# Edges' multiplicity as a logarithm in the logits, maxima of four heads at once, and two of four heads set apart by GpSimd, in a graph attention softmax

## The reference, cut to what matters

```python
x = x * jax.lax.rsqrt(ms + EPS) * rms_w
x = x @ W_down
loop = jnp.arange(n, dtype=edge_index.dtype)
src = jnp.concatenate([edge_index[0], loop])
dst = jnp.concatenate([edge_index[1], loop])
xl = (x @ Wl).reshape(n, H, D)          # H = 4 heads, D = 64
xr = (x @ Wr).reshape(n, H, D)
msg = xl[src] + xr[dst]
act = jnp.where(msg > 0, msg, NEG_SLOPE * msg)
e = jnp.einsum('ehd,hd->eh', act, att)
m = jax.ops.segment_max(e, dst, num_segments=n)
p = jnp.exp(e - m[dst])
denom = jax.ops.segment_sum(p, dst, num_segments=n)
alpha = p / (denom[dst] + 1e-16)
out = jax.ops.segment_sum(alpha[..., None] * xl[src], dst, num_segments=n)
out = out.reshape(n, HID)
return out @ W_up
```

## Time and profile before

| | |
|---|---|
| median of 3 runs | 3800.36 us (3797.71 to 3806.73) |
| the profiled execution | 3811.61 us |
| its span in the trace | 3809.9 us |
| granted TensorE clock, mean | 0.956 of full speed |
| busy: TensorE (matmul) | 3487.1 us, 92% |
| busy: TensorE (weight loads) | 2907.5 us, 76% |
| busy: VectorE | 1925.3 us, 51% |
| busy: GpSimd | 1237.3 us, 32% |
| busy: ScalarE | 904.2 us, 24% |
| chain that ended last | TensorE 60%, DMA 12%, GpSimd 10%, VectorE 7%, issue 6%, ScalarE 4% |
| in it: scatter into EM, its DMA | 6% |
| in it: exponentials L1908 | 2% |

### The profile page before, as it was taken

The page is one execution under the profiler, slowest core; times in us unless marked ns, Lnnn a source line. Parts: engine busy times, 40 slices in busy tenths (PEclk is TensorE's granted clock), DMA queues, the critical chain, the costliest instruction groups (busy, mean ns, idle before and its releaser), DMA issues.

```text
span 3809.9 us, 55179 instructions
## 1 busy us (share of the span) xinstructions
PE 3487.1 (92%) x22747; PEld 2907.5 (76%) x22747; DVE 1925.3 (51%) x4210; ACT 904.2 (24%) x1340; POOL 1237.3 (32%) x947
## 2 busy tenths in 40 slices
PE   5899079999999799999999699999999999999988
PEld 4665058999999799987778596777777777777788
DVE  7864155221333354455545497676764444444467
ACT  0111024111201211221111394332312222222224
POOL 2677633322333027776677562200000000000021
PEclk8999589999999899999999899999999999999999
DMA  8588862556422435455544557442341222221233
GB/s 291 140 263 244 244 201 65 131 126 142 121 59 51 167 102 161 153 169 185 164 145 144 185 218 269 173 139 81 123 141 56 90 76 81 77 87 67 68 100 104
DMA packets 270889, 533.95 MB, mean 140 GB/s; under 512 B 86587, under 2 KB 135730, under 8 KB 268618
## 3 DMA queue, kind: packets, MB, share of 16 engines
q1 hardware_dynamic: 145526, 400.68, 31.0%
q0 software_dynamic: 74080, 52.74, 8.7%
q10 hardware_dynamic: 51030, 77.00, 5.8%
HBM read 352.66 MB, written 177.63 MB: 139 GB/s over the span
## 4 chain that ended last, share of the span: by engine, by line
PE 60%; DMA 12%; POOL 10%; DVE 7%; issue 6%; ACT 4%; SPq 0%; POOLq 0%; ACTq 0%; DVEq 0%
PE ps L393 40%; PE ps L721 14%; DMA EM<-ee,adr 6%; POOL gr L2151 3%; POOL EM L2141 3%; POOL gl L2151 3%; PE ps L483 3%; DMA T<-cnt,adr 2%; ACT pb L1908 2%; DVE eqj L882 1%; POOL T L2114 1%; DVE eqj L879 1%; DMA slab<-T 1%; PE ps L398 1%; ACT pt L1922 1%
## 5 line engine op out<-in xcount | busy, mean ns | idle before, releaser
L721 PE MATMUL ps<-mh,whl 128*128 128x384 f16 (+5 forms) x2560 | 528.5, 300 | 20.3 <-DVE gs L1391 14.4
L393 PE MATMUL ps<-wb,xth 128*128 128x256 f32 (+1 forms) x2560 | 460.8, 282 | 7.1 <-DVE xtl L1056 5.2
L2114 POOL DMA_INDIRECT TR<-cnt,adr x167 | 270.8, 1621 | 541.2 <-DMA TR<-cnt,adr 509.6
L393 PEld LDWEIGHTS ps<-wb,xth 128*128 128x128 f32 (+1 forms) x2560 | 389.2, 186 | 8.1 <-DVE xtl L1056 5.4
L2189 POOL TENSOR_TENSOR graw<-graw,rsb 128x1280 f32<-128x1280 f32 (+1 forms) x2 | 5.6, 2822 | 1166.8 <-DMA graw<-GD 1166.8
L721 PE MATMUL ps<-ml,whl 128*128 128x384 f16 (+5 forms) x1280 | 383.0, 299 | 0.0
L721 PEld LDWEIGHTS ps<-mh,whl 128*128 128x128 f16 (+1 forms) x2560 | 289.1, 117 | 92.7 <-issue 14.5
L393 PE MATMUL ps<-wb,xtl 128*128 128x256 f32 (+1 forms) x1280 | 358.5, 280 | 0.0
L393 PE MATMUL ps<-a,yy 128*128 128x384 f16 (+4 forms) x2560 | 343.7, 297 | 6.5 <-DVE yy L1403 5.2
L393 PE MATMUL ps<-a,xhb 128*128 128x384 f16 (+5 forms) x1280 | 341.0, 296 | 0.0
L393 PE MATMUL ps<-a,xob 128*128 128x384 f16 (+5 forms) x1280 | 339.8, 296 | 0.0
(11 more groups left out here) (308 smaller groups left out, 6974.1 us busy)
## 6 DMA issues: line engine op xcount, KB each, us to landing
TR<-zero_w SPq DMA_DIRECT2D x80, 625.0 KB, 3.8
wraw<-in_L_gnn_weight SPq DMA_DIRECT2D x64, 512.0 KB, 3.3
EM<-neg SPq DMA_DIRECT2D x10, 2500.0 KB, 21.8
ar<-TR SPq DMA_DIRECT2D x72, 320.0 KB
eb<-EM SPq DMA_DIRECT2D x9, 2500.0 KB, 9.1
ar<-TR SPq DMA_DIRECT2D x72, 305.0 KB
UD<-ue ACTq DMA_DIRECT2D x72, 256.0 KB, 3.2
uu<-UD SPq DMA_DIRECT2D x36, 512.0 KB, 6.9
```

Of the source, the lines that this page charges most:

```text
L393: i = pe.matmul(ap, l, r, start=(q == 0), stop=(q == len(pairs) - 1))
L721: ins = pe.matmul(ps[:, 0:cn], l, r, start=(q == 0), stop=(q == len(pairs) - 1))
L2114: return pool.indirect_dma_start(out=flat, out_offset=bass.IndirectOffsetOnAxis(ap=adr[:, n, t:t + 1], axis=0), in_=cnt[:, n, t:t + 1], in ...
```

## The change

Multiplicity moves from a multiplication of the exponentials into the logits: n exp(e) = exp(e + ln n). For that the kernel fetches the counts: `times` gathers BD at each edge into `cg` (one indirect DMA for each of 167 columns, between the additions to TR), `load_loops` reads BD's diagonal into `dg` (ten strided loads). BD gets one more row of zeros, which the addresses of unused edges reach; VectorE raises cg to at least 1, ScalarE takes the logarithms of both between two tiles of x2T, and VectorE adds them to ed and to ee. The loads of nb, GpSimd's multiplications and `weigh_late` are gone. rms is now computed before and within the loop over x2T.

In the softmax eb gets a third buffer. VectorE takes the maxima of all four heads of a tile at once, after the copies of head 0 of the tile before: three elementwise maxima that halve the 1250 columns each (m1, m2, m3), and one reduction. Tile 0 keeps its four reductions. GpSimd copies the odd heads of eb into pb packed, and ScalarE takes their exponentials in place. VectorE takes over the copy of the second bank out of PSUM from ScalarE. The loads of z3 begin with the upper five tiles.

```diff
@@ buffers
-        eb = [at(f"eb{i}", [128, N, 4], F32, O + 19.75 * i) for i in range(2)]
+        eb = [at(f"eb{i}", [128, N, 4], F32, O + (0, 19.75, 90)[i]) for i in range(3)]
+
+        m1 = at("m1", [128, 625, 4], F32, O + 110)
+        m2 = at("m2", [128, 313, 4], F32, O + 119.875)
+        m3 = at("m3", [128, 157, 4], F32, O + 124.875)
@@ TensorE, a head
-                if h < 3:
-                    w.wait_ge(*G("weighed", i, h))
-                else:
-                    w.wait_ge(*V("weighed", i, h))
+                w.wait_ge(*A("exp", i, h))
@@ VectorE, x2T
             for i in range(NT):
                 turned_rows("x2T", i)
+                if i == 5:
+                    rsqrt(dve, w, rms[:, :], vpe[:, :], t10[:, :], "rms")
+                    w.wait_ge(*cg_in("cg"))
+                    dve.tensor_scalar(out=cg[:, :], in0=cg[:, :], scalar1=1.0, scalar2=None, op0=ALU.max).then_inc(*V.tick("cg"))
@@ VectorE, logits of a batch of edges
+                w.wait_ge(*A("cg"))
+                dve.tensor_tensor(ee[:, t0:t0 + m, :], ee[:, t0:t0 + m, :], cg[:, t0:t0 + m, None].broadcast_to([EP, m, 4]),
+                                  ALU.add).then_inc(*V.tick("ee", b))
@@ VectorE, softmax
+            def maxima(i):
                 r, a = ROWS[i], i % 2
+                w.wait_ge(*em_in[i % 3](i))
+                w.wait_ge(*V.now())
+                dve.tensor_tensor(m1[0:r, :, :], eb[i % 3][0:r, 0:625, :], eb[i % 3][0:r, 625:1250, :], ALU.max).then_inc(*V.tick())
+                w.wait_ge(*V.now())
+                dve.tensor_tensor(m2[0:r, :, :], m1[0:r, 0:313, :], m1[0:r, 312:625, :], ALU.max).then_inc(*V.tick())
+                w.wait_ge(*V.now())
+                dve.tensor_tensor(m3[0:r, :, :], m2[0:r, 0:157, :], m2[0:r, 156:313, :], ALU.max).then_inc(*V.tick())
+                w.wait_ge(*V.now())
                 if i >= 2:
                     w.wait_ge(*A("exp", i - 2, 3))
...
+                dve.tensor_reduce(out=mx[0:r, a, :], in_=m3[0:r, :, :].rearrange("p s h -> p h s"), axis=AX.X, op=ALU.max,
+                                  negate=True).then_inc(*t)
@@ VectorE, a head
+                n = (3 * g + 1) % NPT
+                w.wait_ge(*P("pt", i, h, 1))
+                if 3 * g + 1 >= NPT:
+                    w.wait_ge(*P("att", *heads[(3 * g + 1 - NPT) // 3]))
+                dve.tensor_copy(pt[n][:, :, 0:r], four(psum.at("pt", i, h, 1), r)).then_inc(*psum.taken_out(V, "pt", i, h, 1))
...
-                if h == 1:
-                    weigh_late(i)
-                if i + 1 < NT:
-                    maxima(i + 1, h)
+                if i + 1 < NT and h == 0:
+                    maxima(i + 1)
@@ ScalarE, x2T
+                if i == 1:
+                    root_of(rms[:, :], vpe[:, :], V("rmsv"), "rms")
...
+                if i == 7:
+
+                    w.wait_ge(*dg_in("dg"))
+                    for r, c in ((128, slice(0, 9)), (98, slice(9, 10))):
+                        act.activation(dg[0:r, c], dg[0:r, c], ACT.Ln).then_inc(*A.tick("dg"))
+                    w.wait_ge(*V("cg"))
+                    act.activation(cg[:, :], cg[:, :], ACT.Ln).then_inc(*A.tick("cg"))
@@ ScalarE, exponentials
-                act.activation(pb[n][0:r, :], eb[a][0:r, :, h], ACT.Exp, bias=mx[0:r, a, h:h + 1]).then_inc(*A.tick("exp", i, h))
+                if h % 2:
+                    w.wait_ge(*G("apart", i, h))
+                act.activation(pb[n][0:r, :], pb[n][0:r, :] if h % 2 else eb[i % 3][0:r, :, h], ACT.Exp, bias=mx[0:r, a, h:h + 1]).then_inc(*A.tick("exp", i, h))
@@ GpSimd, additions to TR
             for t in range(ET):
                 w.wait_ge(*tr_add.now())
                 w.wait_ge(*V("adr", 1, min(t // 34 * 34 + 33, ET - 1)))
                 add_counts(TR, 1, t, RPAD * N - 1).then_inc(*tr_add.tick("last"))
+                for c in range(*((t - 20, t - 19) if t < 147 else (2 * t - 167, 2 * t - 165))):
+                    if c >= 0:
+                        times(c)
@@ GpSimd, softmax
-            for i, h in heads:
-                if h < 3:
-                    r, a, n = ROWS[i], i % 2, (4 * i + h) % 6
-                    w.wait_ge(*A("exp", i, h))
-                    w.wait_ge(*bd_in[a](i))
-                    pool.tensor_tensor(pb[n][0:r, :], pb[n][0:r, :], nb[a][0:r, :], ALU.mult).then_inc(*G.tick("weighed", i, h))
+            for g, (i, h) in enumerate(heads):
+                if h % 2:
+
+                    r = ROWS[i]
+                    w.wait_ge(*em_in[i % 3](i))
+                    if g >= 6:
+                        w.wait_ge(*P("pt", *heads[g - 6], 2))
+                    pool.tensor_copy(pb[g % 6][0:r, :], eb[i % 3][0:r, :, h]).then_inc(*G.tick("apart", i, h))
@@ SP
+            def load_loops():
+                w.wait_ge(*V("rsqrt", "dis"))
+                for i in range(NT):
+                    a0, r = 128 * i * (N + 1), ROWS[i]
+                    sp.dma_start(dg[0:r, i:i + 1], BD.rearrange("a b -> (a b)").rearrange("(c d) -> c d", d=1)[
+                        a0:a0 + (r - 1) * (N + 1) + 1:N + 1, :], allow_slow_non_contiguous=True).then_inc(*dg_in.tick("dg"))
```

More of the change, by code:

```diff
@@ L330, in program @@
         rd = at("rd", [128, 2, 4], F32, O + 69.5625)
-        nb = [at(f"nb{i}", [128, N], F32, 1 + 5 * i) for i in range(2)]
         z3 = [at(f"z3{i}", [128, D], F32, O + 4 * i) for i in range(NT)]
@@ L1146, in vector @@
                                       ALU.subtract).then_inc(*V.tick("wds"))
-            w.wait_ge(*V.now())
-            dve.tensor_tensor(t10[:, :], rsd[:, :], rsd[:, :], ALU.mult).then_inc(*V.tick())
-            w.wait_ge(*V.now())
-            dve.tensor_tensor(t10[:, :], t10[:, :], mvb[:, :, 1], ALU.mult).then_inc(*V.tick())
-            w.wait_ge(*V.now())
-            dve.tensor_scalar(out=vpe[:, :], in0=t10[:, :], scalar1=RMS_EPS, scalar2=None, op0=ALU.add).then_inc(*V.tick("rmsv"))
-            rsqrt(dve, w, rms[:, :], vpe[:, :], t10[:, :], "rms")
             w.wait_ge(*V.now())
@@ L1193, in vector @@
                 w.wait_ge(*V.now())
+                dve.tensor_reduce(out=ed[0:r, i0:i1, :].rearrange("p m h -> p (m h)"),
+                                  in_=zz_.rearrange("p m (h d) -> p (m h) d", h=4), axis=AX.X, op=ALU.add).then_inc(*V.tick())
+                w.wait_ge(*V.now())
+                w.wait_ge(*A("dg"))
                 t = V.tick("ed")
@@ L1789, in scalar @@
                 s.at["last",] = s.n
-            root_of(rms[:, :], vpe[:, :], V("rmsv"), "rms")
             def high2(n):
@@ L1914, in scalar @@
                 r = ROWS[i]
[L1915 to L1922 removed]
+                n = 3 * g % NPT
+                w.wait_ge(*P("pt", i, h, 0))
+                if 3 * g >= NPT:
+                    w.wait_ge(*P("att", *heads[(3 * g - NPT) // 3]))
+                t = psum.taken_out(A, "pt", i, h, 0)
+                A.at["pt", i, h] = A.n
+                act.activation(pt[n][:, :, 0:r], four(psum.at("pt", i, h, 0), r), ACT.Copy).then_inc(*t)
                 if g + 3 < len(heads):
@@ L2481, in load3 @@
                     sp.dma_start(wraw[s % 3][:, :, :], tiles3[s]).then_inc(*w3_in[s % 3].tick(s))
-            w.wait_ge(*A("exp", 8, 3))
-            for i in range(NT):
-                if i == 4:
+            w.wait_ge(*A("exp", 7, 3))
+            for i in (5, 6, 7, 8, 9, 0, 1, 2, 3, 4):
+                if i == 9:
+                    w.wait_ge(*A("exp", 8, 3))
+                elif i == 0:
                     w.wait_ge(*A("exp", 9, 3))
```

77 lines of the change are left out of this document (39 added, 38 removed).

## The result

| | before | changed |
|---|---|---|
| median of 20 runs each | 3807.22 us (3797.71 to 3816.58) | 3818.68 us (3812.91 to 3827.33) |
| ratio to before | | 1.0029 [1.0020, 1.0038] |
| span of the profiled execution | 3809.9 us | 3811.9 us |
| granted clock, mean | 0.956 | 0.955 |

The change makes the kernel slower by 0.29%, 11 us (7.6 to 14.5). It was forecast slower, by 8.5 us, at 3808.9 and within 3790 to 3818: the measured time lies 0.7 us above the range. The two profiled executions differ by 2.0 us only, so the first thing to do is to cut them into stages.

The account below looks back on a forecast made before the run. ScalarE and TensorE were both near the bound in the softmax, TensorE with 0.6 us of slack a tile. Terms +8.0 - 1.8 + 1.8 + 0.5 = +8.5 us on 3800.4 gave 3808.9 us, range 3790 to 3818.

Parts of the forecast that it names:

- edit 1: Softmax, steady tile: ScalarE's work falls to 9.9 us, or 12.2 if packing gains nothing, both under TensorE's 13.3.
- edit 3: Softmax, steady tile: GpSimd's copy gets between m1 and m2, tile 14.9 us against 13.91, +8.0 us over eight tiles.
- edit 4: Start of the softmax: no wait for nb, so head 4 starts at 2188.6 instead of 2190.40, -1.8 us.
- edit 5: Between tiles 7 and 8 of x2T: table load and logarithms on ScalarE lie in the path, +1.8 us (1.3 to 2.5).
- edit 6: Before SAGE: ten loads of the diagonal queue ahead of the first weights and delay them, +0.5 us (0 to 3).
- edit 7: Additions to TR: 167 gathers of counts, 1.4 us each, fit GpSimd's idle time of 3.2 us an addition; no cost.
- The third buffer: Softmax logits: a third eb buffer removes no wait of before, since VectorE never waited for eb after the first load.
- The level: Whole kernel: the +8.5 us sum was added to the median of 3800.4 us, giving 3808.9.

Follow-up runs that it names:

- e1: The change without GpSimd's copies, ScalarE reading eb directly for all four heads; ratio to the kernel before 1.0012.
- e2: The change with each GpSimd copy waiting until the maxima of its tile are there; ratio to the kernel before 0.9998.
- e3: The change with the second bank copied out of PSUM by ScalarE again, not VectorE; ratio to the kernel before 1.0031.
- e9: The change with GpSimd's copies waiting for their tile's maxima and the logarithms moved behind x2T; ratio to the kernel before 1.0034.
- e14: The change with GpSimd's copies waiting for their tile's maxima and the logarithms behind x2T, timed a second time; ratio to the kernel before 0.9983.
- e4: The change with the logarithms moved behind x2T and the diagonal's loads behind the first SAGE weights; ratio to the kernel before 1.0028.
- e6: The change with two buffers of logits instead of three and z3's loads in the old order; ratio to the kernel before 1.0055.

## Why the prediction was right, and where it failed

- **ScalarE's sum (edit 1): right, the conclusion not.** Its busy time in the 40 us fell from 40.00 to 25.96, and a packed exponential takes 1.35 us, as taken. But I wrote that reading eb directly would cost nothing, since ScalarE's 12.2 us stay under TensorE's 13.3: in e1 the tile is 13.68, against 13.33 in e2. By e1 and e3 the order of ScalarE's work closes a loop of its own.
- **GpSimd's copy gets into the chain (edit 3): right, place and order.** m1, GpSimd's copy, m2. The copy takes 2.5 us where I took 2.9, by the multiplication's 2.87, and the tile is 14.66 where 14.9 was forecast; seven tiles cost 4.8 us, not 7. This is where the Trainium skill's SBUF — State Buffer, "Who interferes with whom", which I had cited, agrees with the trace: 3.65 us against 1.46 for the pair it names, and in e2 no effect on copies out of PSUM. The estimate of 3.0 us, from the figure in the Trainium skill's GPSIMD Engine Reference, "Performance pitfalls for Q7 kernels", was too high: 2.5 measured.
- **The start (edit 4): wrong, and it is the step that failed.** I forecast that head 4 comes 1.8 us earlier, and that tile 1 costs as much as any other. Head 4 came 0.1 us earlier, head 8 2.2 us later. Up to the end of head 1's copies the reckoning holds to 0.1 us (19.4 us after the first maximum). The term that failed is the next, "1.1 + 2.2 of TensorE until head 4", taken at full clock: it took 4.95 us, not 3.3, and the clock was still at 0.50 for head 4's transposes, 1.0 us more. What I left out is that a hole in TensorE's work costs once as a hole and again as clock: behind all eleven holes of 1.78 to 4.50 us at the start of the softmax, in the change, e1 to e9 and e14, it fell to 0.50. From the first maximum to head 8 the forecast was -0.8 (the start and one tile), the trace says +2.2, and in e4 it was +6.3.
- **The logarithms (edit 5): the mechanism right, the size low in this profile.** 1.6 us of waiting against 1.8 forecast, 0.9 of clock on top. Over the seven kernels with the logarithms at that place the stage takes 60.05 to 61.81 us, 60.7 on average, against 59.1 and 59.7 before, so the typical price is 1.3 us.
- **The loads of the diagonal (edit 6): 0.5 taken, 0.1 measured.** The gathers (edit 7): hidden, as forecast.
- **The third buffer: true of the kernel before, and beside the point.** It removes no wait there, but the change itself would be slower without it (e6).
- **The level.** I added the sum to the median of three runs, 3800.4 us; twenty runs have 3807.2. With 10.2 us for the stages on that, 3817.4 comes out. A range that ends at 3818 had no room for a median that is off by 7 us, although the three runs themselves spread by 9. Of the 9.8 us between forecast and measurement 6.9 are this level, 1.7 the stages, and 1.2 stay open.
- **Luck.** That the stages add to 10.2 us where 8.5 were forecast owes something to luck: the start (3.0 us too low), the logarithms (0.9) and the end of the softmax (0.5, not in the sum) missed on one side, the seven tiles (2.2) and the loads of the diagonal (0.5) on the other.

## What to carry to other kernels

Before a serial chain of two-input VectorE instructions is put beside GpSimd work on SBUF, look where GpSimd's instruction will be released: one semaphore wait that moves it behind the chain was worth 9 us here. For an engine that is no longer the bound, don't sum its work: follow the loop from one release to the next, since a copy behind two exponentials can be late on an engine that is idle a quarter of the time (e3). And count a hole of a few microseconds in TensorE's work at least double, because the heads behind it may run at half the clock: summed over the instructions behind it, the hole of 3.25 us in the change cost 4.2 us more as clock, the 4.40 of e4 nearly 10. A comparison of stages within the traces showed all of this at a size that the times alone could not.
